# Expert tokens moved by indirect DMA instead of one-hot products, in a two-layer attention and expert kernel

## The reference

```python
def _L1_ffn_ref(x, w_router, w_up, w_gate, w_down, ws_up, ws_gate, ws_down):
    logits = x @ w_router
    probs = jax.nn.softmax(logits.astype(jnp.float32), axis=-1).astype(logits.dtype)
    topk_vals, topk_idx = jax.lax.top_k(probs, TOPK)
    up = jnp.einsum('btd,edh->ebth', x, w_up)
    gate = jax.nn.silu(jnp.einsum('btd,edh->ebth', x, w_gate))
    exp_out = jnp.einsum('ebth,ehd->ebtd', up * gate, w_down)
    out = jnp.zeros_like(x)
    eids = jnp.arange(E - 1)
    for i in range(TOPK - 1):
        idx_i = topk_idx[..., i]
        sel = (idx_i[None, :, :] == eids[:, None, None]).astype(x.dtype)
        gathered = jnp.einsum('ebt,ebtd->btd', sel, exp_out)
        out = out + ALPHA * topk_vals[..., i:i + 1] * gathered
    shared = x @ ws_up * jax.nn.silu(x @ ws_gate) @ ws_down
    return out + shared
```

## Time and profile before

| | us |
|---|---|
| median of 3 runs | 343.63 (341.34 to 346.12) |
| the profiled execution, its time | 343.77 |
| its span, first to last instruction | 341.7 |
| PE, DVE, ACT, POOL busy | 291.4, 267.6, 208.9, 152.8 |

### The profile page before, as it was taken

How to read it: one execution, slowest core, us unless ns; L and a number is a source line. 1 busy time by engine, 2 the same in 40 slices (tenths; PEclk the granted TensorE clock), 3 DMA queues, 4 the chain that set the end, 5 groups by cost and what they waited for, 6 DMA issues and landing times.

```text
span 341.7 us, 8943 instructions
## 1 busy us (share of the span) xinstructions
PE 291.4 (85%) x3485; PEld 222.3 (65%) x3485; DVE 267.6 (78%) x698; ACT 208.9 (61%) x442; POOL 152.8 (45%) x157
## 2 busy tenths in 40 slices
PE   5598856389999988999998999775888998999994
PEld 5455745275665744785766787544655997758993
DVE  4789969988674597977999567789699899794832
ACT  3574935335757648896867999234863656844561
POOL 8901848544864030453435355313522656333551
PEclk9999969959999999998999999899899999999999
DMA  7600022532230000000000000000003011031211
GB/s 237 257 2 1 3 94 94 167 110 93 92 133 2 0 0 4 2 2 2 2 2 3 2 2 3 2 0 2 1 3 152 36 60 36 2 140 46 76 54 32
DMA packets 6609, 16.64 MB, mean 49 GB/s; under 512 B 676, under 2 KB 2984, under 8 KB 6568
## 3 DMA queue, kind: packets, MB, share of 16 engines
q1 hardware_dynamic: 6568, 16.08, 13.7%
HBM read 10.83 MB, written 0.52 MB: 33 GB/s over the span
## 4 chain that ended last, share of the span: by engine, by line
PE 51%; DVE 36%; issue 5%; ACT 4%; DMA 1%; POOL 1%; SPq 0%; DVEq 0%; ACTq 0%
PE ps L808 7%; DVE MX L1404 6%; PE ps L810 6%; PE ps L809 6%; PE ps L1037 6%; DVE prl L667 4%; DVE stat L1359 3%; PE ps L1099 3%; PE ps L881 2%; PE ps L869 2%; PE ps L870 2%; DVE pr L1580 2%; PE ps L1129 2%; PE ps L1025 1%; PE ps L961 1%
## 5 line engine op out<-in xcount | busy, mean ns | idle before, releaser
L667 POOL TENSOR_TENSOR prl<-pr,prh 128x384 f16<-128x384 f32 (+1 forms) x48 | 48.5, 1011 | 81.7 <-ACT pr L1188 81.7
L1185 ACT ACTIVATE prh<-ps 128x384 f16<-128x384 f32 (+1 forms) x96 | 51.6, 537 | 20.5 <-PE ps L810 10.3
L1404 DVE TENSOR_REDUCE MX<-ps 128x8 f32<-128x512 f32 (+2 forms) x80 | 51.9, 682 | 8.8 <-PE ps L911 4.5
L672 POOL TENSOR_TENSOR prl<-pr,prh 128x512 f16<-128x512 f32 x28 | 32.9, 1181 | 44.1 <-ACT prh L1225 44.1
L777 POOL TENSOR_TENSOR wl<-wraw,wh 128x512 f16<-128x512 f32 (+1 forms) x30 | 34.7, 1178 | 14.8 <-DVE wh L1292 14.7
L667 DVE TENSOR_TENSOR prl<-ps,prh 128x384 f16<-128x384 f32 (+1 forms) x48 | 28.4, 594 | 5.6 <-ACT ps L1188 5.1
L1580 DVE TENSOR_TENSOR pr<-ps,hr 128x512 f32<-128x512 f32 x28 | 19.0, 685 | 12.5 <-ACT hr L1219 10.8
L819 PE MATMUL ps<-cst 128*128 128x128 f32 x130 | 24.0, 324 | 4.6 <-DMA cst<-in_const 4.1
L1225 ACT CAST prh<-pr 128x512 f16<-128x512 f32 x28 | 17.2, 617 | 15.2 <-DVE pr L1580 15.2
L1188 ACT ACTIVATE ps<-ps 128x384 f32<-128x384 f32 (+1 forms) x48 | 26.1, 543 | 0.0
L1188 ACT ACTIVATE pr<-ps 128x384 f32<-128x384 f32 (+1 forms) x48 | 25.7, 535 | 0.0
(11 more groups left out here) (256 smaller groups left out, 1064.4 us busy)
## 6 DMA issues: line engine op xcount, KB each, us to landing
wraw<-in_weights SPq DMA_DIRECT2D x8, 768.0 KB, 4.2
wraw<-wh SPq DMA_DIRECT2D x6, 384.0 KB, 2.6
wraw<-wl SPq DMA_DIRECT2D x6, 384.0 KB, 3.1
wraw<-in_weights SPq DMA_DIRECT2D x2, 576.0 KB, 7.3
rowb<-in_rows SPq DMA_DIRECT2D x1, 708.0 KB, 5.0
wd<-in_down SPq DMA_DIRECT2D x1, 576.0 KB, 7.4
X<-in_x SPq DMA_DIRECT2D x2, 256.0 KB, 4.8
picks<-in_spread SPq DMA_DIRECT2D x1, 512.0 KB, 5.7
```

Source lines behind the costliest of these rows:

```text
L667: return engine.tensor_tensor(prl[:, g, three, 0:width], whole, prh[:, g, three, 0:width], ALU.subtract)
L672: return engine.tensor_tensor(hlo[:, g, k % NPV, :], hh[:, g, k % 2, :], hhi[:, g, k % NPV, :], ALU.subtract)
L1185: nc.scalar.activation(high, src[:, 0:width], ACT.Exp, scale=SCALE[a]).then_inc(pr_ready, 1)
L1404: nc.vector.tensor_reduce(o, src[:].rearrange("p (h k) -> p h k", h=heads), AX_X, ALU.max).then_inc(max_read, 1)
```

## The change

Tokens now reach their slots through memory. Each group has a table `by_slot[g]` of 1280 rows in DRAM; it is cleared from a tile of zeros (`xs_zero` on POOL, two DMAs from SP), with the number 1024, which is no token, as every row's token. `ln_plain x3` writes its result to `xrow`, where each token has 130 numbers: its 128, its own number (`ids`) and its weight. Four indirect DMAs from POOL for each group (`scatter`) write the rows to the slots in `place`. SP reads the table back to `xslot` in three DMAs, when all four have landed; `sorted` transposes these tiles on PE (fp32) and splits them on ACT and DVE.

On the way back, ACT scales a tile's result by the slot's weight into `y`, a ring of four buffers for each group, and an indirect DMA from POOL (`send`) adds the 128 rows to the output in DRAM at the tokens' numbers; rows with no token are left out by the bounds check. So the output of the group, `x` plus the shared expert, must have been written before (`out_done[g]`), and it is written earlier than before the change, after `add1`. `onehot`, `onehot_t`, `spots`, `sort_high`, `sort_low`, `xsplit`, `back` and the second part of `add1` are gone.

SP's list is now made by the planner too, with the spill weights, the reading back and the output in it. The keys and values of the last attention (`k2`, `vctx 2`) wait for `up0` of k = 5 of group 0. The planner's table has new numbers (two of its lines stand for the rest), and `bias_split` works on three rows at once.

```diff
-GROUP_LEAD = 3.8
+GROUP_LEAD = 3.6
+LANDS = {("scatter", "sorted"): 5.5, ("add1", "send"): 3.0}
...
-    k2 = chain([("stack", "k2", 0, j) for j in range(2)], chain([("nat", "k2", 0)], ("split_low", 2, 2), k0))
+    k2 = chain([("stack", "k2", 0, j) for j in range(2)], chain([("nat", "k2", 0)], ("split_low", 2, 2), k0, ("up0", 0, 5, 0)))
     k2 = chain([("kblocks", 2, 0)], k2, *[("scores", 0, b, 3) for b in range(B)])
-    chain([("vctx", 2)], ("split_low", 2, 2))
+    chain([("vctx", 2)], ("split_low", 2, 2), ("up0", 0, 5, 0))
...
+        placed = chain([("scatter", g, t) for t in range(T)], gate, normed, ("xs_zero",), ("ids",))
+        for j in range(3):
+            chain([("sorted", g, j)], placed, *[("up1", 0, k) for k in users(j)] * g)
...
-                chain([("back", *s)], ("downr", *s), ("onehot_t", g, tile))
-                also(("back", *s), ("back", *line[i - 1]) if i > CH else ("add1", g, 0))
-        chain([("add1", g, 0)], ("down1", g, CH - 1))
-        chain([("add1", g, 1)], ("back", *line[-1]))
+                chain([("send", *s)], ("downr", *s), ("add1", g))
+                if i > CH:
+                    also(("send", *s), ("send", *line[i - 1]))
+        chain([("add1", g)], ("down1", g, CH - 1))
...
+            "masks0": [("act", 1.)], "b3_add": [("pool", 1.27)], "ln_pow": [("pool", 1.5)], "masks1": [("act", .9)], "kbs_zero": [("pool", 3.6)], "bo_add": [("pool", 1.2)], "xs_zero": [("pool", 1.3)], "scatter": [("pool", 1.1)], "send": [("pool", 1.1)], "ids": [("dve", .3)],
+            "sorted": [("pe", .95), ("act", .6), ("dve", .69)]}[k]
...
+            sp.wait_ge(xs_zeroed, 2)
+            for g in range(G):
+                sp.dma_start(by_slot[g].rearrange("(s p) d -> p s d", p=P), xslot[:, 0]).then_inc(slots_zero, 16)
...
+            for e in orders["sp"]:
+                g = e[1]
+                if e[0] == "scatter":
+                    sp.wait_ge(x_placed, 16 * T * (g + 1))
+                    for j in range(3):
+                        tiles = slice(4 * j, min(4 * j + 4, TILES))
+                        sp.dma_start(xslot[:, g, tiles], by_slot[g].rearrange("(s p) d -> p s d", p=P)[:, tiles]).then_inc(in_xslot[j], 16)
+                elif e[0] == "fetch":
+                    fetch_spill(e[1])
+                else:
+                    sp.wait_ge(add_read, nth[e])
+                    sp.dma_start(out.rearrange("(g t p) d -> p g t d", g=G, p=P)[:, g], X[:, g]).then_inc(out_done[g], 16)
...
+                elif kind == "scatter":
+                    _, g, t = e
+                    pool.wait_ge(place_ready, nth[("rank", g)])
+                    pool.wait_ge(plain_done, nth[("ln_plain", "x3", g)])
+                    pool.wait_ge(g1_ready, nth[("gate1", g)])
+                    pool.wait_ge(ids_ready, 1)
+                    pool.wait_ge(slots_zero, 16 * G)
+                    nc.gpsimd.indirect_dma_start(
+                        out=by_slot[g], out_offset=bass.IndirectOffsetOnAxis(ap=place[:, g, t:t + 1], axis=0),
+                        in_=xrow[:, g, t, :], in_offset=None, bounds_check=SLOTS - 1, oob_is_err=False).then_inc(x_placed, 16)
+                elif kind == "send":
+                    _, g, k = e
+                    pool.wait_ge(out_done[g], 16)
+                    pool.wait_ge(y_ready, nth[("downr", g, k)])
+                    nc.gpsimd.indirect_dma_start(
+                        out=out, out_offset=bass.IndirectOffsetOnAxis(ap=token_of[:, g, TILE_ORDER[k - CH], :], axis=0),
+                        in_=y[g][:, (k - CH) % 4, :], in_offset=None, bounds_check=B * S - 1, oob_is_err=False,
+                        compute_op=ALU.add).then_inc(y_sent[g][(k - CH) % 4], 16)
...
+                elif kind == "sorted":
+                    _, g, j = e
+                    pe.wait_ge(in_xslot[j], 16 * (g + 1))
+                    take(bank[e][0], sorted_ready, n)
+                    for i in range(min(4, TILES - 4 * j)):
+                        mm = nc.tensor.transpose(o[:, i * P:(i + 1) * P], xslot[:, g, 4 * j + i, 0:P], ident)
+                    mm.then_inc(sorted_mm, 1)
...
                     if k - CH >= 4:
-                        sc.wait_ge(back_mm, nth[("back", g, k - 4)])
-                    nc.scalar.copy(yhl[g][:, (k - CH) % 4, 0, :], src[:, 0:P]).then_inc(y_high, 1)
+                        sc.wait_ge(y_sent[g][(k - CH) % 4], 16 * ((k - CH) // 4))
+                    nc.scalar.activation(y[g][:, (k - CH) % 4, :], src[:, 0:P], ACT.Identity,
+                                         scale=xslot[:, g, TILE_ORDER[k - CH], P + 1:P + 2]).then_inc(y_ready, 1)
```

More of the change, by code:

```diff
@@ L30 @@
 CONST = {"ident": 0, "tri_q": 128, "tri_k": 256, "signs": 384, "iota": 390, "heads": 398, "experts": 414,
-         "over": 422, "before": 425, "jump": 489, "home": 497, "nth": 505, "part": 508}
-NCONST = 518
+         "over": 422, "before": 425, "jump": 489, "home": 497, "nth": 505, "token": 508}
+NCONST = 516
 ROUTED, SPILL = 7, 3
@@ L144, in experts1 @@
     def experts1(g, normed, turned):
-        chain([("xsplit", g)], normed)
         gate = chain([("gate1", g), ("rank", g)], turned)
-        spots = chain([("onehot", g)], gate, *[("back", 0, CH + TILES - 1)] * g)
-        for j in range(3):
-            for kind in ("sort_high", "sort_low"):
-                chain([(kind, g, j)], spots, ("xsplit", g))
         chain([("spill", g)], gate, *[("spill", 0)] * g)
@@ L153, in experts1 @@
             also(("rank", 1), ("spill", 0))
-        chain([("spots", g)], gate)
-        for s in range(TILES):
-            chain([("onehot_t", g, s)], ("spots", g), *[(kind, g, j) for kind in ("sort_high", "sort_low") for j in range(3)])
+        placed = chain([("scatter", g, t) for t in range(T)], gate, normed, ("xs_zero",), ("ids",))
+        for j in range(3):
+            chain([("sorted", g, j)], placed, *[("up1", 0, k) for k in users(j)] * g)
         line = [(g, k) for k in range(CH + TILES)]
@@ L170, in experts1 @@
                 tile = TILE_ORDER[i - CH]
-                also(("up1", *s), *[(kind, g, tile // 4) for kind in ("sort_high", "sort_low")])
+                also(("up1", *s), ("sorted", g, tile // 4))
                 also(("up1", *s), ("split_low", FIRST1 + 1 + tile if tile < ROUTED else PIECES - 1, 2))
@@ L215, in plow, with users @@
     return ("plow" if u % 2 == 0 else "plow_pool", a, b, u)
+def users(j):
+    return [CH + TILE_ORDER.index(tile) for tile in range(4 * j, min(4 * j + 4, TILES))]
 def spill_of(g, k):
@@ L273, in group @@
     if e[0] in ("gate0", "gate1", "spread", "up0", "up1", "hi1", "lo1", "down0", "down1", "add0", "add1", "bo_add", "b3_add",
-                "xsplit", "rank", "onehot", "sort_high", "sort_low", "spots", "onehot_t", "downr", "back", "spill"):
+                "rank", "sorted", "scatter", "send", "downr", "spill"):
         return e[1]
@@ L288, in banks_of @@
     return int(e[0] in ("max", "scores", "up0", "ctx", "vctx", "nat", "stack", "turn", "square", "v1", "negmax", "gate0", "gate1",
-                        "spread", "rank", "sort_high", "sort_low", "spots", "downr"))
+                        "spread", "rank", "sorted", "downr"))
 def schedule():
@@ L335, in schedule @@
     order = {engine: [] for engine in clock}
+    order["sp"] = []
     first, taken = {}, {}
@@ L374, in schedule @@
             if e[0] == "downr" and s == 1 and e[2] - CH >= 4:
-                needed += [(("back", e[1], e[2] - 4), 0)]
+                needed += [(("send", e[1], e[2] - 4), 0)]
+                fetched = end.get(needed[-1], 0.0) + 3.0
             if engine == "pe":
@@ L408, in schedule @@
         last = s + 1 == len(stages[e])
+        if last and (e[0] == "scatter" and e[2] == T - 1 or e[0] == "add1"):
+            order["sp"].append(e)
+        if e[0] in ("spill", "downr"):
+            order["sp"] += [("fetch", n) for n in range(SPILL * G) if ("fetch", n) not in order["sp"]
+                            and (("spill", n // SPILL), 0) in end and (n < 2 or (("downr", *spill_step(n - 2)), 0) in end)]
         if not last:
@@ L492, in build @@
         pos = sb("pos", [P, T])
[L493 removed]
+        place = sb("place", [P, G, T], I32)
         cmp8 = sb("cmp8", [P, 3, 8])
@@ L1118, in _ @@
                     mm.then_inc(downr_mm, 1)
-                elif kind == "back":
-                    _, g, k = e
-                    s = TILE_ORDER[k - CH]
-                    pe.wait_ge(y_ready, nth[("downr", g, k)])
-                    pe.wait_ge(onehot_t_ready, nth[("onehot_t", g, s)])
-                    if k == CH:
-                        take(bank[e][0], add_read, nth[("add1", g, 1)])
-                    for t in range(T):
-                        tt = slice(t * P, (t + 1) * P)
-                        for a in range(2):
-                            mm = nc.tensor.matmul(o[:, tt], onehot_t[:, s, tt], yhl[g][:, (k - CH) % 4, a, :],
-                                                  start=(k == CH and t == 0 and a == 0),
```

(2 more changed lines are left out.)

188 lines of the change are left out of this document (62 added, 126 removed).

## The result

| kernel | median us | lowest to highest | runs | ratio to before, 95% |
|---|---|---|---|---|
| before | 343.73 | 341.34 to 346.12 | 4 | |
| after | 361.75 | 360.28 to 362.59 | 4 | 1.052, 1.044 to 1.060 |

The changed kernel is 5.2% slower. Forecast were 346 us, with a range from 338 to 357. Its profiled execution took 362.59 us with a span of 360.5.

A forecast was written before the change was run, and what follows sets the result against it. PE bounds the last 53 us before; after, POOL ends last: 281.7 + 27.8 + 24 issues at 1.1 (26.4) + 6 + 2.3 = 344.2, plus 2.07 around the span, gives 346 us, range 338 to 357.

The forecast's parts named there:

- s: POOL's time to issue one scatter or send, 24 in stretch two's sum; shown by no row, taken as 1.1 us.
- the POOL sum of stretch two: From group 1's turn of x3 to the end: 281.7 + 27.8 + 24 s + 6 + 2.3 = 344.2 us, POOL last.
- PE's sum: PE's work from group 1's turn of x3 to the end, with bare tail and last send: ends at 340.1 us.
- Stretch one: Up to group 1's turn of x3: gain between 0 and 6.9 us, taken as 3, so the turn at 281.7.
- added 9.0, gone 9.0: inside, nothing: Inside group 1's chain: gate, rank and sorted subtractions added; compares, onehot_t, low parts and some hidden products gone; no net change.
- Group 0's round trip: Slots through memory, near 10 us against some 6 us of matmuls; PE waits about 4 us, not added.
- The third rival: Scatter brings nothing: group 0's wait for tiles drags group 1's chain, stretch one gains 0, 349 us; chance 0.08.
- The removed work: Busy time saved across the kernel: PE about 15 us, DVE over 20 us, POOL two xsplit of about 1.16.
- k2 later: Last attention's k2 moved behind group 0's first experts; slack of over 100 us, costed at nothing.
- The landing: At the end, 2.3 us for a send; an accumulating one well over that would hold ACT through the four-buffer ring.
- One: Expert stages: PE sets the pace, s 0.9 or less; 342 us at 0.20, 332 to 337 with whole shift at 0.13.
- Two: Both expert stages: issues cost more than they look, everything waits for POOL; s over 1.35 at 0.25, s = 1.5 gives 355.9.

The follow-up runs named there:

- Experiment 2: The changed kernel with its 20 sends written as plain indirect writes, without the addition: 351.0 us, ratio 1.021 to before.
- experiment 11: The changed kernel with group 0's 10 sends taken out and group 1's 10 kept: 357.85 us, ratio 1.044 to before.
- experiment 1: The changed kernel with its 20 sends and the waits for their landing taken out: 345.58 us, ratio 0.9997 to before.
- 12: The changed kernel with each send adding only 64 of the 128 columns of each row: 364.33 us, ratio 1.057 to before.
- experiment 4: The kernel before with only k2 and vctx 2 held back behind group 0's sixth up0 step: 343.23 us, ratio 0.998.
- 10: The kernel before with the factor for idle filler matmuls on PE raised from 1.6 to 3.2: 344.71 us, ratio 1.004.
- experiment 13: The changed kernel without sends, the factor for idle filler matmuls on PE raised from 1.6 to 3.2: 341.47 us, ratio 0.990 to before.
- experiment 6: The changed kernel without sends, its sorting transposes also not waiting for the way through memory: 342.86 us, ratio 0.994 to before.
- experiment 3: The changed kernel with all 24 lo1 subtractions moved from POOL to DVE, all sends kept: 348.17 us, ratio 1.014 to before.

## Why the prediction was wrong, point by point

**The step that failed** is the value of s in the POOL sum of stretch two: "I take 1.1, next to POOL's own streaming instruction of 1.16". Measured are 1.29 us for a scatter and 1.86 for a send. Then 24 s becomes 4 x 1.29 + 20 x 1.86 = 42.4 instead of 26.4, and the sum 344.2 + 16.0 = 360.2; the span was 360.5. The mechanism, POOL last and PE hidden beneath it, was the forecast one, and the term was mis-sized. Experiment 2 bears the sum out at another s: with plain sends it gives 317.8 + 24 x 1.29 = 348.8, and the span was 348.8 (its turn of x3 came at 280.29, 1.4 us ahead of the sum's). Two reasons lie in the text itself. It took one s for two kinds of issue, and the value that it took fits the plain one fairly (0.99 + 0.30). And it asked what the addition would do to the landing and not what it does to the issue, which experiment 2 puts at 0.57 us each. Its bounds, 0.4 and 2.3, did hold both; the range stopped at s = 1.55 and had to leave out the case that came true, to which 0.25 was given.

**That the sum agreed is partly luck.** The start was 1.9 us late. From there POOL's own work, with the 0.17 and 0.30 us between instructions, took 68.2 us where 27.8 and 42.4 make 70.2, since an issue behind a subtraction follows sooner than one behind an issue. The waiting was 6.9 us in six gaps (1.29, 0.91, 0.53, 1.52, 0.41 and 2.21), where the sum allowed 6, and from the end of the last send to the end it was 1.8 instead of 2.3. The sum also counts each issue alike, and experiment 11 shows that group 0's ten sends cost some 3 us and not 18.6. A sum that begins at group 1's first send would have been the better one.

**PE's sum** was 4 us short. Without the send and its landing it gives 47.0 + 3.8 + 4.9 = 55.7 us from the turn of x3 to the end; the kernels without sends took 60.0 and 337.2 - 277.65 = 59.6. The kernel before took 57.0. What PE was freed of did not shorten the stretch; in experiment 1 PE waits 5.9 us for `lo1` there.

**Stretch one** was forecast to move the turn of x3 from 284.66 to 281.7; it came at 283.60. Behind that small miss lie two large ones of opposite sign. The chain started 10.7 us sooner, more than the "up to 6.9", for which the prediction shows no working; and "added 9.0, gone 9.0: inside, nothing" was wrong by 9.6 us, since from reciprocal to turn it took 39.0 us instead of 29.4. That length hardly varies: 38.8 to 39.2 us in the five kernels with the same work up to the turn (after and experiments 1, 2, 11 and 12), and 29.4 before and in experiments 4 and 10. The start does vary, from 241.12 to 248.19 in the same five, and the turn with it, from 280.29 to 287.31. A reading of one turn to 2 us is worth little.

The length went up in one place. These are rows of DVE in the first normalisation, before and then after:

```profile
260.02 0.69 DVE L1443 TENSOR_SCALAR act<-ps 128x512 f32<-128x512 f32 x1 [0.30 <-PE ps L895]
...
263.12 1.14 DVE L1377 SCALAR_TENSOR_TENSOR lnx<-act,mv,rowb 128x128 f32<-128x128 f32 x4
...
265.11 1.12 DVE L1391 SCALAR_TENSOR_TENSOR lnx<-lnx,rstd,rowb 128x128 f32<-128x128 f32 x4
```

```profile
251.52 0.69 DVE L1448 TENSOR_SCALAR act<-ps 128x512 f32<-128x512 f32 x1 [0.28 <-PE ps L933]
...
253.75 0.19 DVE L1484 TENSOR_REDUCE r<-ps 128x4 f32<-128x32 f32 x1 [0.22 <-PE ps L1043]
...
259.24 2.98 DVE L1382 SCALAR_TENSOR_TENSOR lnx<-act,mv,rowb 128x128 f32<-128x128 f32 x4
262.14 0.17 DVE L1508 TENSOR_TENSOR cmp<-ps,cst 128x24 f32<-128x24 f32 x1
...
264.59 1.14 DVE L1396 SCALAR_TENSOR_TENSOR lnx<-lnx,rstd,rowb 128x128 f32<-128x128 f32 x4
```

From the projection's result (the first row of each) to the last step of the normalisation (the last row) it is 5.1 us before and 13.1 after: 8.0 of the 9.6 us. Group 0's gate (from L1484), two hidden products and group 0's rank (from L1508) now stand between them, and the step between the two takes 2.98 us instead of 1.14. What had left DVE gave little back: from the reciprocal to the projection's result the chain takes 7.0 us instead of 4.8, although the compares are gone, and from the next product's result (270.58 before, 270.24 after) to the turn 13.4 instead of 14.1. So the step that failed in this stretch is the balance of busy times: what was put into the chain counted, what was taken out had mostly not held it up. The lower clock, which the prediction named and did not add ("may find a lower clock afterwards"), came earlier than it said, ahead of the round trip: 0.60 between 245 and 260 us and 0.80 up to 285 (1.00 in both before). It has the smaller part: with the clock at 1.00 and 0.93 in experiment 13 the chain still takes 36.5 us, and the normalisation 11.4 of them (247.15 to 258.55). That the sort's absence is what thinned PE there is argued, not shown.

**Group 0's round trip** was rightly not added. PE waited 0.5 us for the slots in after, and at most 4.6 at a time in the other kernels that wait for them, but group 1's chain is as long without that wait (38.7 us, experiment 6) as with it. The third rival fell with this: stretch one gained 1.1 us instead of 3, for another reason.

**The removed work**: DVE's busy time fell by 21.8 us, as forecast (over 20). PE's 15 us do not show in its busy time, which rose by 0.9, since at a lower clock fewer instructions are busy for as long: between 245 and 260 us 73 matmuls at 0.60 for 13.8 us in after, and 148 at 1.00 for 13.3 before.

**k2 later** at nothing was right (experiment 4).

**The landing** of a send is 3.1 us at the median and 2.3 without the addition, by the profiles' lists of DMAs; the ring of four buffers held ACT twice, for 2.7 us together. That was named as a risk and is small: the end came 3.4 us after the last send began.

**The rivals.** One (s of 0.9 or less) fell. Two came true, in place and direction; with the measured 42.4 us its own formula gives 362.3 us. The reason that it gave for a high s did not. The Trainium skill's rule that GpSimd can't write descriptors while DVE is in a 2-port mode ("SBUF — State Buffer", SBUF: two separate sides) was weighed there as the way to it. The sends took 1.56 us with DVE idle, as at the end of after, so the price needs no lock. A lock of that kind does show in experiment 3: five of the 20 sends, those that began with 0.3 us or more of a subtraction on DVE still to run, took 0.24 to 0.47 us more. That subtraction takes 0.69 us, as long as DVE's product from PSUM, so no row says that it is in a 2-port mode; but the same section of the Trainium skill also names a DVE operation with two SBUF inputs, against a GpSimd operation that reads SBUF, and this one has two (`pr` and `prh`). All 20 sends together held GpSimd for 32.8 us there and for 31.3 in after.

The Trainium skill's figure of about 1 us to the first byte of a software-made DMA ("DMA: Bandwidth & Descriptors", Specifications) was used as an estimate for s and gave 343.9 us. No row shows the first byte; the traces have 2.3 to 3.1 us to the landing and 0.99 to 1.56 us of GpSimd's own time; a latency is no occupancy, and the latter was what the sum needed.

## What to carry to other kernels

When a change hands work to an engine through DMA issues that no trace has yet shown, price each kind of issue by itself and put a micro-measurement or a wide bound in its place: here a 128-row scatter held GpSimd for 0.99 us, the same with an addition for 1.56, plus 0.30 between two. Count such a queue from the moment when the last group's first result exists, and look who else needs a place in it; moving `lo1` off it returned 13.1 of the 18.0 us. Do not set busy time that leaves a chain against busy time that enters it: ask for each piece whether the chain waited for it. Here gate and rank, moved into the chain, made it 8 us longer in one place, and what had left made it hardly shorter. And look at TensorE's granted clock where its work has been taken away: it fell from 1.00 to 0.60 here.

## What the runs showed of the hardware

- An indirect DMA from GpSimd with addition: 1.56 us, also with half the bytes in a row; without it 0.99 us; 0.30 us until the next issue may begin, 0.17 after a subtraction. 144 packets against 32.
- An issue with addition that began with 0.3 us or more of a DVE subtraction from SBUF still to run took 1.80 to 2.03 us instead of 1.56 (experiment 3).
- DVE can be held by POOL for 2.3 us. In after, two small operations on SBUF that take 0.35 and 0.19 us in the kernel without sends ended only with a `lo1` that stood behind a send:

```profile
297.59 1.56 POOL L820 DMA_INDIRECT out<-act,xslot  x1 [0.53 <-issue]
298.62 1.72 POOL L678 TENSOR_TENSOR prl<-pr,prh 128x512 f16<-128x512 f32 x1
```

```profile
298.08 2.32 DVE L1518 TENSOR_TENSOR zz<-zz,cst 128x32 f32<-128x32 f32 x1
```

The other is at 291.87, 2.25 us. The issue alone does not hold DVE: in experiment 3, where no subtraction stands behind it, a send runs from 293.21 to 294.76 us, and DVE's operations on SBUF that start inside it at 293.72 and 293.94 take 0.18 and 0.19 us. As far as these rows show, it takes the subtraction in the queue behind the issue.
